# One destination product per quad, a shared tail for the last two batches, and the first block's chain among the table products of a graph layer

## The reference

```
msg  = concat(x[dst], edge_attr)                # 64 + 64 features per edge
h    = relu(msg @ W1a.T + b1a) @ W1b.T + b1b    # 128 hidden, 64 out
agg  = segment_sum(h, src) / max(count(src), 1)
z    = relu(concat(x, agg) @ W2a.T + b2a) @ W2b.T + b2b
out  = concat(z, x) @ Wr.T + br
return layernorm(x + out)                       # without scale and shift
```

## Time and profile before

| | us |
|---|---|
| median of 3 runs | 1608.92 (1605.97 to 1609.6) |
| the profiled execution | 1609.42 |
| its span | 1607.3 |
| PE busy | 1552.7 (97%) |
| DVE busy | 1404.1 (87%) |
| ACT busy | 941.7 (59%) |
| POOL busy | 1152.0 (72%) |

### The profile page before, as it was taken

One profiled execution on the slowest core, in us unless ns is written; L12 is line 12 of the kernel. 1 busy time (PEld: TensorE's weight loads), 2 busy tenths in 40 slices (PEclk: granted clock), 3 DMA queues, 4 the chain that ended last, 5 costly groups with the idle time before them and its releaser, 6 DMA issues.

```text
span 1607.3 us, 42297 instructions
## 1 busy us (share of the span) xinstructions
PE 1552.7 (97%) x13755; PEld 1276.8 (79%) x13755; DVE 1404.1 (87%) x3954; ACT 941.7 (59%) x1808; POOL 1152.0 (72%) x929
## 2 busy tenths in 40 slices
PE   9899999999999999999999999999999999995996
PEld 6578878878887888878878887888888888884885
DVE  5599998999999999999999988999999999884885
ACT  2376767767676776767767674555455554563222
POOL 2277777777777777777877788788788877876451
PEclk9899999999999999999999999999999999997998
DMA  8265655656666566556666669889989898866996
GB/s 253 72 168 159 171 157 162 175 156 169 161 164 166 163 160 167 165 163 164 162 163 166 166 167 305 270 273 290 289 278 284 267 296 273 275 174 219 347 370 198
DMA packets 135500, 335.22 MB, mean 209 GB/s; under 512 B 36506, under 2 KB 69565, under 8 KB 129016
## 3 DMA queue, kind: packets, MB, share of 16 engines
q0 software_dynamic: 53184, 224.62, 43.1%
q1 hardware_dynamic: 80740, 102.43, 26.2%
q10 hardware_dynamic: 1364, 5.49, 1.2%
HBM read 212.88 MB, written 119.52 MB: 207 GB/s over the span
## 4 chain that ended last, share of the span: by engine, by line
PE 84%; DMA 5%; DVE 4%; POOL 2%; issue 2%; ACT 1%; SPq 0%; POOLq 0%; DVEq 0%; ACTq 0%
PE HH L523 22%; PE MS L532 18%; PE PA L548 13%; PE PBk L548 13%; PE RK L561 7%; DMA gbuf<-region,idx 4%; PE RK L640 2%; PE RK L645 2%; PE PA L561 2%; PE CK L608 2%; POOL region L1261 1%; DVE OH L1103 1%; PE RK L657 1%; POOL gbuf L1289 1%; DVE M L983 0%
## 5 line engine op out<-in xcount | busy, mean ns | idle before, releaser
L1261 POOL DMA_INDIRECT region<-stg,dest x806 | 1010.5, 1254 | 349.6 <-issue 181.6
L532 PE MATMUL MS<-W,hT 128*128 128x64 f32 x3224 | 507.9, 258 | 1.3 <-DVE T L1117 0.8
L532 PEld LDWEIGHTS MS<-W,hT 128*128 128x128 f32 x3224 | 467.1, 191 | 3.6 <-issue 2.5
L523 PE MATMUL HH<-eab,pw 128*128 128x512 f32 x806 | 434.7, 621 | 3.3 <-ACT hT L782 2.6
L983 DVE TENSOR_SCALAR M<-pos_of,pos 128x384 bf16<-128x384 int16 x1612 | 404.4, 309 | 0.0
L548 PE MATMUL PA<-Z,M 128*128 128x195 bf16 x2418 | 353.9, 254 | 6.5 <-ACT stg L828 2.6
L828 ACT ACTIVATE stg<-PA 120x585 bf16<-120x585 f32 x403 | 266.4, 661 | 156.8 <-PE PA L548 156.3
L548 PE MATMUL PBk<-Z,M 128*128 128x195 bf16 x2418 | 353.9, 254 | 0.2 <-ACT stg L828 0.2
L548 PEld LDWEIGHTS PA<-Z,M 128*128 128x128 bf16 x2418 | 229.1, 106 | 123.9 <-issue 118.9
L782 ACT ACTIVATE hT<-HH 128x512 f32<-128x512 f32 x403 | 240.8, 597 | 137.3 <-PE HH L523 137.3
L828 ACT ACTIVATE stg<-PBk 120x585 bf16<-120x585 f32 x403 | 265.9, 660 | 52.1 <-PE PBk L548 50.3
(11 more groups left out here) (199 smaller groups left out, 1543.3 us busy)
## 6 DMA issues: line engine op xcount, KB each, us to landing
eab<-in_ea SPq DMA_DIRECT2D x201, 256.0 KB
kb<-keyd SPq DMA_DIRECT2D x201, 128.0 KB
pw<-ptab SPq DMA_DIRECT2D x403, 32.0 KB
region<-stg,dest POOLq DMA_INDIRECT x806
gbuf<-in_xt ACTq DMA_DIRECT2D x6, 422.5 KB
ptab<-OH SPq DMA_DIRECT2D x7, 256.0 KB, 3.3
gbuf<-region,idx POOLq DMA_INDIRECT x98, 8.5
eab<-in_xt SPq DMA_DIRECT2D x12, 130.0 KB
```

Source lines behind the costliest of these rows:

```text
L523: e.matmul(HH[:, :], pw[:, q % 4, :], eab[:, c % NB, at_q:at_q + GE], start=True, stop=True).then_inc(s_h, 1)
L532: ins = e.matmul(MS[:, o:o + D], hT[:, q % 2, 128 * j:128 * j + 128], W[:, W_1B:W_1B + D], start=True, stop=True)
L1261: e.indirect_dma_start(region[s], bass.IndirectOffsetOnAxis(ap=dest[:, g:g + 1], axis=0), stw[:, g % NS, :], None).then_inc(s_sc[g % NS], 16)
```

## The change

- **One destination product.** The two groups of a quad now lie in the two halves of the partitions: group 0 in rows 0 to 49, group 1 in rows 64 to 113 of `offs2`, `S` and `Dz`. `stair` builds one staircase of 120 columns per quad over 128 partitions instead of two over 50. `Dz` has its columns masked by `C_HALF`, so that one matmul with six columns gives both groups. The block's chain has one small matmul more and its first step (L1016) multiplies by the mask.
- **The head.** Slots -44 to -7 stand among the table products by the table `AMID` (after product n all slots below `AMID[n]`), ACT's chain copies with them. `front` is now each turn its own two quads, so quad 0 starts in turn 0. Chunk loads 1 and 2 and the loads of the larger part of the index arrays `dc`, `sc` (all but the columns of the first two blocks) are moved: the latter from ACT's queue in the prologue to SP's queue behind the windows of quads 2 and 3. The constants array grows from 1319 to 1701 columns.
- **The tail.** Batch 12 (`END`) has buffers of its own for x, for the input and for the middle of the node network, and the second bank of `PA` for its product; its x is loaded before the quad loop's last wait. The steps of batch 11 and 12 stand side by side.

```diff
-CHAIN = -6
+AMID = {3: -38, 4: -30, 5: -22, 6: -13, 7: -11, 8: -10, 9: -9, 10: -8, 11: -7, 12: -6}
...
-                e.dma_start(dc[:, FEW:NT], dstc[:, FEW:NT]).then_inc(p_rest, 16)
-                e.dma_start(sc[:, FEW:NT], srcc[:, FEW:NT]).then_inc(p_rest, 16)
...
-        front = {-3: 0, -1: 1, **{m: m for m in range(2, NP)}}
+        front = {m: m for m in range(NP)}
...
-                        if n in (4, 7, 10):
-                            load_chunk((n - 4) // 3)
+                        if n == 4:
+                            load_chunk(0)
                     e.wait_ge(s_pt, 16 * PB)
                     for c in range(NP):
-                        if c >= NB:
+                        if c:
                             load_chunk(c)
                         for q in range(CQ * c, CQ * c + quads_of(c)):
                             load_window(q)
+                        if c == 1:
+                            e.dma_start(dc[:, FEW:NT], dstc[:, FEW:NT]).then_inc(s_rest, 16)
+                            e.dma_start(sc[:, FEW:NT], srcc[:, FEW:NT]).then_inc(s_rest, 16)
...
-                            e.matmul(RK[0:CL, Q_OFF:Q_OFF + BG], tri50[:, :], kcb[:, :], start=True, stop=True)
+                            e.matmul(RK[0:64, Q_OFF:Q_OFF + BQ], tri50[:, :], kcb[:, 0::2], start=True, stop=True)
+                            e.matmul(RK[64:128, Q_OFF:Q_OFF + BQ], tri50[:, :], kcb[:, 1::2], start=True, stop=True)
...
-                            for g in range(2):
-                                k = 2 * (q % BQ) + g
-                                at_g = Q_DEST + 3 * ((2 * q + g) % 8)
-                                last = e.matmul(RK[:, at_g:at_g + 3], S[:, q % 4, g, :],
-                                                Dzb[:, b % 2, :, 2 * k + 1], start=True, stop=True)
+                            k = 4 * (q % BQ)
+                            at_q = Q_DEST + 6 * (q % 4)
+                            last = e.matmul(RK[:, at_q:at_q + 6].rearrange("p (k g) -> p k g", g=2), S[:, q % 4, :],
+                                            Dzb[:, b % 2, :, k + 1:k + 4:2], start=True, stop=True)
...
                         spin(e, HH, 4)
-
-                    e.wait_ge(s_bc, 1)
-                    for m in TURNS:
+                        if n == 3:
+                            e.wait_ge(s_bc, 1)
+                        while slot < AMID.get(n, slot):
+                            rank(slot)
+                            slot += 1
+
+                    for m in range(slot // 2, NP + 2):
...
-                        e.tensor_tensor(S[0:CL, q % 4:q % 4 + of_pair(m), :, 0:KC].rearrange(
-                                            "p q g (n u) -> p (q g) n u", u=2),
+                        e.tensor_tensor(S[:, q % 4:q % 4 + n, 0:KC].rearrange("p q (n u) -> p q n u", u=2),
...
-                    for n in range((NC - 1 - 6) // 4, NBAT):
-                        if n > (NC - 1 - 6) // 4:
-                            turn(n)
-                        if n > (NC - 1 - 7) // 4:
-                            first(n)
-                        if n > (NC - 1 - 8) // 4:
-                            second(n)
+                    for n in range((NC - 1 - 6) // 4 + 1, NBAT):
+                        turn(n)
+                    for n in range((NC - 1 - 7) // 4 + 1, NBAT):
+                        first(n)
+                    for n in range((NC - 1 - 8) // 4 + 1, NBAT):
+                        second(n)
```

More of the change, by code:

```diff
@@ L236, in bank4 @@
             return (PA, PBk)[n // 2 % 2][:, 512 * (n % 2):512 * (n % 2) + 512]
-        (p_c, p_w, p_sc, p_f, p_g, p_v, p_k, p_t, p_s, p_one, p_rest) = [sem(f"p{i}") for i in range(11)]
+        (p_c, p_w, p_sc, p_f, p_g, p_v, p_k, p_t, p_s, p_one) = [sem(f"p{i}") for i in range(10)]
         p_xt = [sem(f"p_xt{k}") for k in range(4)]
@@ L372, in program @@
         s_kw = [sem(f"s_kw{i}") for i in range(4)]
-        s_nx = [sem(f"s_nx{i}") for i in range(2)]
+        s_nx = [sem(f"s_nx{i}") for i in range(3)]
         s_ob = [sem(f"s_ob{i}") for i in range(3)]
-        s_xo = [sem(f"s_xo{i}") for i in range(2)]
+        s_xo = [sem(f"s_xo{i}") for i in range(3)]
         (s_key, s_dg, s_bb, s_bc, s_zz,
@@ L378, in program @@
          s_oh, s_h, s_relu, s_msg, s_x, s_r, s_l, s_M, s_pA, s_pB, s_eA, s_eB,
-         s_OHv, s_acc, s_ad, s_nt, s_tx, s_zt, s_z1, s_r1, s_y, s_sq, s_var, s_rt, s_fin, s_sw, s_zr, s_zs, s_id, s_P, s_pz, s_pt, s_xr) = [
-            sem(f"s{i}") for i in range(46)]
+         s_OHv, s_acc, s_ad, s_nt, s_tx, s_zt, s_z1, s_r1, s_y, s_sq, s_var, s_rt, s_fin, s_sw, s_zr, s_zs, s_id, s_P, s_pz, s_pt, s_xr, s_rest) = [
+            sem(f"s{i}") for i in range(47)]
         again = [*s_ch, *s_pw, *s_sc, *s_ga, *s_gb, *s_tab, *s_kw, *s_nx, *s_ob, *s_xo,
@@ L671, in rank @@
                         last.then_inc(s_rk, 1)
+                    slot = 2 * FIRST
                     for n in range(PB):
@@ L749, in second @@
                             p = slice(128 * k, 128 * k + 128)
-                            e.matmul(o, z1[:, n % 2, p], Wc[:, :], start=True, stop=False)
-                            last = e.matmul(o, xo[:, n % 2, p], WRX[:, :], start=False, stop=True)
+                            e.matmul(o, node_mid(n)[:, p], Wc[:, :], start=True, stop=False)
+                            last = e.matmul(o, x_rows(n)[:, p], WRX[:, :], start=False, stop=True)
                         last.then_inc(s_y, 1)
@@ L835, in _ @@
                         e.activation(pz(n)[:, 0:w], bank4(n)[:, 0:w], ACT.Copy).then_inc(s_pz, 1)
-                    for m in TURNS:
+                        for i in range(AMID.get(n - 1, 2 * FIRST), AMID.get(n, 2 * FIRST)):
+                            copy_chain(i)
+                    for m in range(AMID[PB - 1] // 2, NP + 2):
                         f = front.get(m)
@@ L870, in relu2 @@
                             e.wait_ge(s_y, n - 1)
-                        e.activation(z1[:, n % 2, 0:w], HH[:, 0:w], ACT.Relu,
+                        e.activation(node_mid(n)[:, 0:w], middle(n)[:, 0:w], ACT.Relu,
                                      bias=W[:, W_B2A:W_B2A + 1]).then_inc(s_r1, 1)
@@ L897, in _ @@
                             n = (c - after) // 4
-                            if c >= after and (c - after) % 4 == 0 and n < NBAT:
+                            if c >= after and (c - after) % 4 == 0 and n < END:
                                 step(n)
+                            if n == END - 1 and (c - after) % 4 == 0:
+                                step(END)
                     e.wait_ge(s_xr, 64)
@@ L1247, in _ @@
                         mean(n)
-                    for n in range((NC - 1 - 10) // 4 + 1, NBAT):
+                    for n in range((NC - 1 - 10) // 4 + 1, END - 1):
                         variance(n)
                         finish(n)
+                    variance(END - 1)
+                    variance(END)
+                    finish(END - 1)
+                    finish(END)
                 @block.gpsimd
@@ L1311, in constants @@
     c[:, C_ROT:C_ROT + BG] = 128.0 * (np.arange(BG) % NROT)
-    c[0:CL, C_DIFF:C_DIFF + CL] = np.eye(CL) - np.eye(CL, k=1)
+    for half in range(2):
+        c[0:CL, C_DIFF2 + 64 * half:C_DIFF2 + 64 * half + CL] = np.eye(CL) - np.eye(CL, k=1)
+        c[64 * half:64 * half + CL, C_HALF + half:C_HALF + BG:2] = 1.0
+        c[0, C_FIRST + 64 * half] = 1.0
     for s in range(NSEG):
@@ L1321, in constants @@
     c[:, C_TRI:C_TRI + 128] = np.triu(np.ones((128, 128)), 1) + BIG * np.eye(128)
+    c[0:CL, C_TRI64:C_TRI64 + 64] = np.triu(np.ones((CL, 64)), 1)
     c[0:CL, C_TRI50:C_TRI50 + CL] = np.triu(np.ones((CL, CL)), 1)
```

103 lines of the change are left out of this document (60 added, 43 removed).

## The result

The changed kernel takes 1583.39 us, median of 4 runs (1581.32 to 1587.88). The kernel before, in its 4 runs, takes 1607.45 (1605.31 to 1609.6). The ratio is 0.9845, 95% interval 0.9824 to 0.9865: 25 us less, give or take 3. The profiled execution took 1581.64 us; PE is still the bound.

What follows compares the result with a forecast made beforehand. PE's issue bounds ordinary turns, latency the program's two ends. 9.9 (product) + 1 (DVE) + 10 (head) + 4.5 (tail) = 25.4 us off the profiled 1609.4 gives 1584, or 1583.5 for a median; range 1575 to 1592.

Steps and rivals of the forecast that it cites:

- Ordinary turns: Quad-loop turns bound by PE's issue: 6.11 us instead of 6.16, removing 403 products at 0.0275 us, 11.1 us in all.
- Part 1 as a whole: Quad loop, one destination product and staircase per quad: 9.9 us from PE plus 1 us from DVE's shorter staircase.
- DVE's relief: Quad loop: shorter staircases take 25 us off DVE, but only 1 us of it counts, in the chain's turns.
- the waits and the longer chain: Turns with a block's chain: 1.2 us lost again to PE waiting for DVE; the chain's added steps below 0.5 us.
- The constants, +1.0: Head: the constants array, 191 KB larger, lands later and delays PE's and DVE's prologue work by 1.0 us.
- Product 12 near 36, first L543 at 43.6, turn 2 at 57.1: Head: times of the last table product, first hidden product and first full turn (before 67.07), a gain of 10 us.
- The stall rival: Head: chunk 2 and windows wait behind the indices, or table stores come later; gain 5 instead of 10, 1588.5; chance 0.15.
- The tail: Program end: batch 12's node network runs beside batch 11's, last finish 0.4 us behind it; 4.5 us gained, 3.5 to 5.
- Bare loads: Quad loop: 0.10 us of weight load per quad comes to stand in the open; slower, 1634; chance 0.03.
- the load price: Quad loop: each pair's removal is worth more, up to half of its printed 0.20 us; 1554; chance 0.03.
- The pair was nearly free: Quad loop: removing the pair gains little, as the following weight load takes its slot; 1592; chance 0.06.
- DVE's relief counts: Chain's turns: the shorter staircase shortens them too, 5 us more, and the head's gain is 12; 1577; chance 0.10.

Runs made afterwards that it cites:

- wide_stair_again: Changed kernel with DVE's staircase 480 columns wide again, one product per quad kept, second run: 1581.75 us, 0.9843 of the kernel before.
- pair_only: Kernel before with only the one destination product and one staircase per quad, larger constants included: 1594.27 us, ratio 0.9908 to the kernel before.
- twice_product: Changed kernel with each destination product issued twice, word for word the same: 1589.76 us, 0.9874 of the kernel before.
- late_rest: Changed kernel with the two 682 KB index loads issued behind the windows of chunk 4 instead of chunk 1: 1576.17 us, 0.9791 of the kernel before.
- head_only: Kernel before with only the head's change (slots among table products, own quads per turn, moved loads): 1595.49 us, ratio 0.9914 to the kernel before.

## Why the prediction was right, and where only its sum was

The prediction was right: 1583.5 foretold, 1583.39 measured, faster, and inside the range of 1575 to 1592. That the two agree to 0.1 us is luck: errors of 1 to 4 us in the terms cancel, as the list shows, and some runs of the same kernel lie 6 us apart. The terms came out like this, from the profiled pair and the parts alone.

- **Ordinary turns, 6.11 for 6.16.** As read from the distance of starts: 0.053 us a turn, and 0.026 a product when it was put back. By the load's price in the Trainium skill ("TensorE: Matmul & The Clock Gate", "LDWEIGHTS (loading the stationary operand)"), 107 ns for 128 columns, an estimate would be four times that; the trace doesn't agree with it as the price of a product in this stream.
- **Part 1 as a whole: 10.9 foretold, 12.1 in these two stretches.** Two errors cancelled. In turns 10 to 144 the ordinary turn gives 134 x 0.053 = 7.1 us, and only 4.7 arrived: one or two turns of each block are 0.1 to 0.2 us longer than before, net of DVE's relief. With that relief at 1.9 us (wide_stair_again) the waits and the longer chain took back 4.3; I had priced them at 1.2 and below 0.5. The chain's turns were also misread: not all of what they have more is PE waiting for DVE. In the kernel before, turns 41, 42 and 43 are 0.9, 0.7 and 0.6 us over an ordinary one; in 42 it is the wait behind the destination product (0.6), in 41 and 43 mostly the chain's own products on PE, and those of 43 went from 0.48 to 0.72 us. In the second phase 7.4 us came where 57 turns x 0.053 make 3.0. The other 4.4 are the waits of PE (5.8 us before, 1.5 now) behind POOL's gathers and in the class sums, which I had not looked at: the prediction has no term for the length of POOL's scatters or the time of its gathers.
- **DVE's relief: 1 foretold, 2 found** in turns 10 to 144, though of the 25 us that DVE was to lose only 8 left it.
- **The constants, +1.0: nothing in the profiled pair.** The array landed 9.0 us after its issue though it is 191 KB larger (850.5 KB instead of 659.5), and DVE's first copy from it starts at 11.07 instead of 11.22. It is not because the index loads had left the prologue: in pair_only, where they had not, that copy starts at 11.23. Over all profiles the term is between: 659.5 KB landed in 8.2 to 9.3 us (three), 850.5 KB in 8.8 to 9.5 (seven), in 10.6 to 11.2 on the slower chip told of above, and once, in twice_product, in 12.5, with PE waiting for it. The issues (KB each, us to landing) of the changed kernel, to the earlier trace rows:

```profile
C<-in_c SPq DMA_DIRECT2D x1, 850.5 KB, 9.0
dc<-in_dstc SPq DMA_DIRECT2D x1, 682.0 KB, 4.7
```

- **Product 12 near 36, first L543 at 43.6, turn 2 at 57.1:** 35.97, 42.79 and 57.45. The last product and the gain of 10 (9.6) stand. The way from turn 0 to 2 was 14.7 and not 13.5. Without the stall it is 11.4 (late_rest), so the latency was priced 2.1 us too long, and the stall on chunk 2's keys behind the indices, 3.3, had no term: that the two nearly cancel is luck. The stall rival came true in part, 3.5 us by turn 2 and 5.0 by turn 10.
- **What the prediction left out of the head is the clock.** It explained the old head's 24.9 us by latency alone. The rows had L523 products at 1.10 and 1.58 us for two, and that difference was the sign. The old head took 24.9, 24.1 and 31.3 us in three profiled executions, the longest with the clock down; the kernel before took 1603.38 to 1615.71 us in its runs beside head_only, head_only 1594.83 to 1597.03.
- **The tail: 4.5 foretold, 4.2 found** (18.1 to 13.95), the last finish 0.34 us behind batch 11's, near the 0.4 forecast. But it is 4.2 or some 1.5, by where the clock falls, so that the profiled pair had the full 4.2 is luck too, and timed alone the part can't be told from nothing.
- **Rivals.** Bare loads and the load price are excluded by twice_product. "The pair was nearly free" is excluded by the same run. "DVE's relief counts" had 5 us, of which 2 were found.

## What to carry to other kernels

Price a short matmul in a stream without waits by the distance of starts around it: here the printed duration of one (0.17 us) overstates its 0.026 us six times, and its load (0.11 us) four times. Where PE waits for transfers or for another engine, read the granted clock beside the waits: a wait of 1.7 us cost 2 to 2.7 us with the clock up, one of 2.3 us with the clock down behind it 5.0. When one engine waits for another's copy, read also what that other engine stood for just before: here it was a transfer that had nothing to do with the copy. Put large loads that nobody needs soon behind the small ones that the next turns want; in one queue they stand ahead of them.

The fastest kernel of this study is the changed one with the index loads behind chunk 4: 1576.17 us, 0.9791 (0.9771 to 0.9810) of the kernel before.

## What the runs showed of the hardware, unexpected

- The same code's head ran with PE's granted clock at 1.00 but for three falls of 3.4 us in one execution, and at 0.50 from 40.6 to 74.7 us in another; turn 2 came at 67.07 and at 73.00.
- One staircase instruction of 480 columns, two of 240 or one of 240 leave POOL's scatters at 1.05 to 1.09 us in the first 560, where the kernel before has 1.19, and each of these kernels has the one product. At the same time DVE's one-hots got longer (L961 to L990: 0.80 to 0.86 us a chunk). What in the product part (the places of rows in two halves, its sums, or where it puts DVE's work beside the scatters) shortens the scatters by 0.1 us stays open.
- On one chip the kernel before and the three others timed there took some 13% longer. The three profiles have a granted clock of 0.97 over the span and a median turn of 6.99 to 7.22 us instead of 6.12, with idle time between engines throughout, while single products take as long as elsewhere (L552 0.26 us on average, L568 0.25 to 0.26).
